# Attention rows: the output product in a score bank behind the turning, the keys copied by VectorE

## The reference

```python
x = _layernorm(pair_rep, gamma, beta)
q = x @ Wq * C ** (-0.5)
k = (x @ Wk).reshape(n, s, s, H, C)
v = (x @ Wv).reshape(n, s, s, H, C)
dpa = jnp.einsum('nsqhc,nsvhc->nsqvh', k, q)
pair_bias = x @ Wb
dpa = dpa + bias[:, None, :, :, None]
attention = jax.nn.softmax(dpa + pair_bias[:, None], axis=3)
out = jnp.einsum('nsqvh,nsvhc->nsqhc', attention, v)
fu = jax.nn.sigmoid(x @ Wu + bu)
out = out * fu
out = out.reshape(n, s, s, H * C) @ Wo + bo
out = out * mask[..., None]
```

## Time and profile before

| | us |
|---|---|
| median of 3 runs | 2528.18 (2527.36 to 2529.87) |
| profiled execution, its own time | 2533.66 |
| its span in the trace | 2531.9 |
| attention rows (76 to 428 us of the span) | 352 |
| PE busy, whole span | 2199.2 |
| DVE busy, whole span | 2185.8 |
| ACT busy, whole span | 1763.2 |
| POOL busy, whole span | 2075.4 |

### The profile page before, as it was taken

One profiled execution on the slowest core, in us unless ns is written; L12 is line 12 of the kernel. 1 busy time (PEld: TensorE's weight loads), 2 busy tenths in 40 slices (PEclk: granted clock), 3 DMA queues, 4 the chain that ended last, 5 costly groups with the idle time before them and its releaser, 6 DMA issues. The chain is left out here.

```text
span 2531.9 us, 36914 instructions
## 1 busy us (share of the span) xinstructions
PE 2199.2 (87%) x9081; PEld 1134.5 (45%) x9158; DVE 2185.8 (86%) x2247; ACT 1763.2 (70%) x3999; POOL 2075.4 (82%) x1330
## 2 busy tenths in 40 slices
PE   6899997776898889988999889999899999988798
PEld 6566664463444444444444333333344333333543
DVE  5677777535999999999999999999999999998796
ACT  4799997566878778787788755656555656553487
POOL 4455555204999999999999999999999999999489
PEclk9999998786999999999999999999989999989899
DMA  4000000005677766776676777777777767765022
GB/s 71 14 12 12 12 12 8 1 1 139 214 232 227 225 232 223 236 226 224 228 228 234 234 241 247 239 231 241 237 230 246 241 231 243 237 224 183 13 60 63
DMA packets 192552, 421.07 MB, mean 166 GB/s; under 512 B 66548, under 2 KB 95705, under 8 KB 192474
## 3 DMA queue, kind: packets, MB, share of 16 engines
q1 hardware_dynamic: 190938, 416.01, 52.1%
q10 hardware_dynamic: 1536, 4.20, 0.5%
HBM read 387.63 MB, written 24.12 MB: 163 GB/s over the span
## 5 line engine op out<-in xcount | busy, mean ns | idle before, releaser
L1589 POOL TENSOR_TENSOR s_hc<-s_h,s_cc 128x1024 f32<-128x1024 f32 x512 | 1200.8, 2363 | 61.2 <-PE s_py L1342 45.4
L1342 PE MATMUL s_py<-s_hc,ident 128*128 128x512 f32 x2048 | 991.6, 609 | 14.9 <-DVE s_yo L1635 14.5
L1672 DVE TENSOR_TENSOR_SCAN s_h<-s_dA,s_state,s_pu 128x1024 f32<-128x1024 f32 x330 | 770.3, 2342 | 27.7 <-PE s_pu L1320 4.7
L1342 PEld LDWEIGHTS s_py<-s_hc,ident 128*128 128x128 f32 x2048 | 389.9, 195 | 386.5 <-issue 314.6
L1503 ACT ACTIVATE s_dA<-s_dt,ss_A 128x1024 f32<-128x1024 f32 x352 | 401.6, 1142 | 9.2 <-ACT s_brow L1459 7.8
L1508 ACT ACTIVATE s_pu<-s_dt,ss_A 128x1024 f32<-128x1024 f32 x160 | 178.4, 1115 | 322.5 <-DVE s_h L1672 317.0
L1582 POOL TENSOR_TENSOR s_dbx<-s_dtx,s_bb 128x1024 f32<-128x1024 f32 x160 | 377.8, 2362 | 2.5 <-DVE s_dtx L1627 2.5
L1672 DVE TENSOR_TENSOR_SCAN s_h<-s_pu,s_state,s_dbx 128x1024 f32<-128x1024 f32 x150 | 350.2, 2335 | 21.2 <-ACT s_pu L1508 19.8
L1648 DVE TENSOR_TENSOR s_pu<-s_pu,s_dtx 128x1024 f32<-128x1024 f32 x288 | 349.1, 1212 | 15.8 <-PE s_pu L1329 13.5
L1329 PE MATMUL s_pu<-s_bcs,ss_sel 128*128 128x512 bf16 x499 | 163.5, 398 | 121.4 <-DVE s_h L1672 117.2
L588 POOL TENSOR_TENSOR ar_ex<-ar_ex,ar_rs 128x512 f32<-128x512 f32 x128 | 133.0, 1039 | 158.3 <-DVE ar_rs L537 158.2
(11 more groups left out here) (289 smaller groups left out, 3587.0 us busy)
## 6 DMA issues: line engine op xcount, KB each, us to landing
s_cc<-rows_scratch SPq DMA_DIRECT2D x512, 512.0 KB, 4.6
s_bb<-rows_scratch SPq DMA_DIRECT2D x160, 512.0 KB, 4.9
s_n<-n_scratch SPq DMA_DIRECT2D x64, 258.0 KB, 5.6
y_scratch<-s_yo SPq DMA_DIRECT2D x16, 512.0 KB, 5.4
s_yf<-y_scratch SPq DMA_DIRECT2D x16, 512.0 KB, 5.8
x_tok<-in_x_dram SPq DMA_DIRECT2D x16, 256.0 KB, 4.5
at_xg<-at_xT SPq DMA_DIRECT2D x64, 64.0 KB, 2.1
n_scratch<-ss_turned SPq DMA_DIRECT2D x32, 128.0 KB, 4.2
```

The source lines that it names most:

```text
L1342: ins = nc.tensor.matmul(p_y[:, hf], lhsT=c.ident[:, :], rhs=hc[:, s % RING, hf], start=(s == 0), stop=(s == U - 1))
L1589: nc.gpsimd.tensor_tensor(hc[:, s % RING, :], h[:, s % RING, :], cc[:, s % C_RING, :], ALU.mult).then_inc(read, 1)
L1672: nc.vector.tensor_tensor_scan(out=flow(h[:, s % RING, :]), data0=flow(decays), data1=flow(inputs), initial=begun, op0=ALU.mult, op1=ALU.a ...
```

## The change

y moves from `ps_o` to the first score bank: `ps_s[:, 0, 128:192]`. With that `attend` no longer waits for `x_done`, `score` waits for the `x_done` of row r-6, since it writes into y's bank, and `project_output` waits for `added` of its own step, since DVE's addition of the bias reads that bank. `project_output` stands right behind `turn`, ahead of `values` and of the projection. On DVE, `add_to_x` works on row r-5 in place of r-6 and stands behind `apply_gate`, ahead of the reciprocal. `take_k` moves from ACT, position 3, to DVE, position 2, behind `take_values`.

```diff
--- before.py
+++ after.py
@@ -417,7 +417,7 @@
         ps_t = ctx.enter_context(nc.psum_tensor("ar_pst", [128, 512], F32))
         ps_o = ctx.enter_context(nc.psum_tensor("ar_pso", [128, 512], F32))
         p_s = ps_s[:, :, 0:128]
-        o_T, p_y = ps_o[:, 0:128], ps_o[:, 128:128 + D]
+        o_T, p_y = ps_o[:, 0:128], ps_s[:, 0, 128:128 + D]
         sem = lambda n: c.sem("ar_" + n)
 
         (q_made, k_made, u_made, q_taken, k_taken, u_taken) = (
@@ -461,8 +461,10 @@
                 nc.tensor.matmul(ps_p[:, :], lhsT=wvu[:, 128:256], rhs=xg[:, k, :], start=True,
                                  stop=True).then_inc(u_made, 1)
 
-            def project_output(r, j, next_attended):
-                pe.wait_ge(gated, r + 2 if next_attended else r + 1)
+            def project_output(r, j, scores_read):
+                pe.wait_ge(gated, r + 1)
+                if scores_read is not None:
+                    pe.wait_ge(added, scores_read + 1)
                 need(pe, x_done, r)
                 nc.tensor.matmul(p_y, lhsT=og[:, j % 2, :], rhs=wo[:, :], start=True, stop=True).then_inc(y_made, 1)
 
@@ -489,7 +491,6 @@
                 pe.wait_ge(e_taken, r + 1)
                 pe.wait_ge(v_taken, r + 1)
                 need(pe, gated, r)
-                need(pe, x_done, r - 1)
                 for h in range(HEADS):
                     ins = nc.tensor.matmul(ps_o[band[h], 0:128], lhsT=va[:, k, j, band[h]], rhs=exT[:, j % 2, tile(h)],
                                            start=True, stop=True)
@@ -499,11 +500,14 @@
 
                 if has(0):
                     need(pe, added, r)
+                    need(pe, x_done, r - 5)
                     score(r, j, g, k)
                 if has(4):
                     attend(r - 4, j, 1 - k)
                 if has(3):
                     turn(r - 3, (j - 3) % GR)
+                if has(5):
+                    project_output(r - 5, (j - 5) % GR, r if has(0) else None)
                 if has(0):
                     values(r, j, k)
                 if pair is not None:
@@ -513,8 +517,6 @@
                         project_k(g + 1, 1 - k)
                     if j == 3:
                         project_u(g + 1, 1 - k)
-                if has(5):
-                    project_output(r - 5, (j - 5) % GR, has(4))
             project_q(0, 0, 0)
             project_k(0, 0)
             project_u(0, 0)
@@ -550,23 +552,31 @@
                 nc.vector.scalar_tensor_tensor(out=xr, in0=p_y, scalar=maskT[:, bass.ds(r, 1)], in1=xr,
                                                op0=ALU.mult, op1=ALU.add).then_inc(x_done, 1)
 
+            def take_k(g, k):
+                dve.wait_ge(k_made, g + 1)
+                need(dve, scored, GR * (g - 1))
+                nc.vector.tensor_copy(kT[:, k, :], ps_p[:, :]).then_inc(k_taken, 1)
+
             def take_values(r, j, k):
                 dve.wait_ge(v_made, r + 1)
                 need(dve, o_made, r - 2 * GR + 1)
                 nc.vector.tensor_copy(va[:, k, j, :], ps_v[:, 0:128]).then_inc(v_taken, 1)
 
             def step(r, j, g, k, has, pair):
-                if has(6):
-                    add_to_x(r - 6)
                 if has(0):
                     add_bias(r, j)
                 if has(4):
                     apply_gate(r - 4, j, g - 1, 1 - k)
+                if has(5):
+                    add_to_x(r - 5)
                 if has(2):
                     invert_sums(r - 2, (j - 2) % GR)
                 if has(0):
                     minimum(r, j)
                     take_values(r, j, k)
+                if pair is not None and j == 2:
+                    take_k(g + 1, 1 - k)
+            take_k(0, 0)
             row_steps(dve, step)
             dve.wait_ge(x_done, S)
 
@@ -603,11 +613,6 @@
                 need(act, scored, GR * (g - 1))
                 nc.scalar.activation(qT[:, k, :], ps_p[:, :], ACT.Copy, scale=-SCALE).then_inc(q_taken, 1)
 
-            def take_k(g, k):
-                act.wait_ge(k_made, g + 1)
-                need(act, scored, GR * (g - 1))
-                nc.scalar.copy(kT[:, k, :], ps_p[:, :]).then_inc(k_taken, 1)
-
             def take_u(g, k):
                 act.wait_ge(u_made, g + 1)
                 need(act, gated, GR * (g - 1))
@@ -634,12 +639,9 @@
                     take_u(g, k)
                 if pair is not None and j == 2:
                     take_q(g + 1, 1 - k)
-                if pair is not None and j == 3:
-                    take_k(g + 1, 1 - k)
                 if has(3):
                     take_turned(r - 3, (j - 3) % GR)
             take_q(0, 0)
-            take_k(0, 0)
             take_u(0, 0)
             row_steps(act, step)
```

## The result

| | before | after |
|---|---|---|
| median, us (4 runs each) | 2529.02 | 2564.02 |
| range of the runs, us | 2527.36 to 2532.20 | 2562.90 to 2566.23 |
| ratio, 95% interval | | 1.0138 (1.0120 to 1.0155) |
| span of the profiled execution, us | 2531.9 | 2561.3 |
| last addition to x of the attention rows ends, us | 427.4 | 459.7 |

The attention rows end 32.3 us later. Of that, 30 groups at 1.01 us are 30 us. The drain, from the start of the last scores to the start of the last addition to x, takes 13.6 us instead of 11.2. The remainder of the program, from that start on, has the same instructions and took 2104.8 us in the profiled execution of before and 2101.9 in that of after, so the two spans differ by 29.4 us. In the twelve other profiled executions of this study that remainder lies between 2095.7 and 2107.1 us, 11 us apart.

What follows compares the result with a forecast made beforehand. In the attention row loop neither PE nor ACT alone was taken as the bound; a ring of waits would lengthen 30 groups from 10.86 to 11.79 us, 28 us, less 1: +27 on 2528.18 gives 2555 us, range 2537 to 2565.

Steps and rivals of the forecast that it cites:

- the ring: Attention row loop: closed chain of waits over four rows through PE, DVE, POOL and ACT, 11.79 us against 10.86.
- (a): DVE to PE: from the start of the bias addition (L528) to the output product that waits for it, 0.81 us.
- (b): On PE: from the output product through values and projection to the next scores, 1.34 us.
- (c): PE and DVE: from scores through the bias addition (L528) to output, 1.38 us at position 2 or 1.47 at 0.
- (d): From output through DVE's addition to x and reciprocal, POOL's scaling and PE's turn to the next output, 2.64 us.
- (e): From output through DVE's addition to x and minimum, ACT's exponentials and q copy to PE's k projection, 3.84 us.
- (f): From PE's k projection through DVE's keys copy to the next bias addition (L528), 1.69 us.
- POOL's ring: Row loop: the output-to-output path through POOL's scaling repeated at all four positions, 4 x 2.64 = 10.56 us a group.
- Rival B: Row loop: q is taken in time, so DVE's own way decides; group 11.27 us, +12 us, 2540; chance 0.14.
- the ceiling: Attend's wait for the addition to x: removing 0.24 us for each of 128 rows gains at most about 30 us.
- Rival C: Row loop: the removed wait wins, k and q copies never late; group 10.56 us, -9 us, 2519; chance 0.08.
- Rival E (the clock): Attention stage: more PE idle time lowers the granted clock, adding 24 us or more, 2580; chance 0.06.

Runs made afterwards that it cites:

- e3: The changed kernel with DVE's addition to x moved behind the reciprocal, still ahead of the minimum: 2554.80 us, 1.0103 of the kernel before.
- e5: The changed kernel with ACT's q copy moved ahead of the exponentials at position 2: 2550.36 us, 1.0069 of the kernel before.
- e4: The changed kernel with DVE's addition to x moved behind reciprocal and minimum, ahead of the values copy: 2538.55 us, 1.0036 of the kernel before.
- e2: The changed kernel with the keys copy put back on ACT at position 3: 2560.01 us, 1.0119 of the kernel before.
- e12: The changed kernel with the addition to x behind the minimum and the keys copy back on ACT: 2533.04 us, 1.0017 of the kernel before.
- e6: The changed kernel with y back in its old bank, the new orders kept: 2579.37 us, 1.0187 of the kernel before.
- e9: The kernel before with turn ahead of attend, DVE's reciprocal ahead of the bias addition, and ACT's four copies ahead of the exponentials: 2529.50 us, ratio 0.9991.
- e10: The kernel before with only the output product moved ahead of the projection, behind values: 2519.79 us, ratio 0.9960.
- e7: The kernel before with only the values product moved ahead of attend and turn on PE: 2529.88 us, ratio 0.9997.

## Why the prediction was right, and where it was off

**The sign, the ring and its members held.** 2555 was forecast with 2537 to 2565; 2564 was measured. The size is less good than that sounds: 2564 is 1 us inside the range and 1 us above the band that I gave to my own case (2545 to 2563), and 35 us were measured where 27 were forecast. All of the waits that I named are there, that of the k projection with 0.5 us in 30 cases where I had 0.6 in 31. One sign of being wrong showed by its letter: the minimum starts 0.29 us behind the addition to x (206.24 to 206.53) and I had written 0.3. The legs had 0.31 there, so the bound was drawn too tight; the waits behind it are as forecast. The ring's sum was 11.79 us a group and the trace has 11.87. Leg by leg, from the rows of after:

| leg | forecast | measured |
|---|---|---|
| (a) L528 to output, position 3 | 0.81 | 0.73 (211.17 to 211.90) |
| (b) output to the scores of position 0 | 1.34 | 1.51 (211.90 to 213.41) |
| (c) scores to output, position 0 | 1.47 | 1.40 (213.41 to 214.81) |
| (d) through POOL to output, position 1 | 2.64 | 2.72 (214.81 to 217.53) |
| (e) through ACT to the k projection | 3.84 | 3.74 (205.66 to 209.40) |
| (f) through the keys copy to L528 | 1.69 | 1.77 (209.40 to 211.17) |
| sum | 11.79 | 11.87 |

That the sum is within 0.08 us is in part luck, since errors of both signs, up to 0.17 us in a leg, cancel. In (a) the wake-up is 0.05 and not 0.12: the weight load itself waits. In (b) output to values is 0.28, values to projection 0.27 and projection to scores 0.96, where the earlier trace rows gave 0.26, 0.22 and 0.86 for other neighbours. In (d) output to the addition to x is 0.68 at a step where output had waited, 0.58 otherwise. The unknown price, the keys copy on DVE, was estimated at 0.68 and is 0.69; the next instruction follows after 0.61, not 0.60.

**The groups and the drain.** 30 groups were right; at 1.01 us they give 30 us. The last step of the sum failed: I took 1 us off for the start and the drain, and the drain is 2.4 us longer. Each drained row of after passes through POOL's ring too: its turns start 2.48, 2.49 and 3.09 us apart (446.97, 449.45, 451.94 and 455.03, each held by POOL), where those of before start 2.03, 1.87 and 1.86 apart (416.96 to 422.72). Of these 2.3 us the ring has 1.7. The other 0.6 is the clock: the last of the three steps runs at the lower level and takes 3.09 instead of 2.49, all of it in PE's own work (the turn shows as 1.11 us instead of 0.65). In before the clock kept its higher level through those steps and fell only behind them, at about 425 us (stretch, busy us, clock, DMA; before, then after):

```profile
410.00:422.00 12.00, 9.97 (x124) 7.36 (x124) 9.31 (x31) 10.52 (x45) 8.64 (x18) 1.00 0.01 2
422.00:428.00 6.00, 3.10 (x26) 2.09 (x26) 1.65 (x6) 0.72 (x2) 0.81 (x2) 0.75 0.01 3
```

```profile
440.00:451.00 11.00, 7.82 (x92) 5.50 (x90) 7.62 (x26) 9.89 (x42) 6.43 (x13) 1.00 0.00 0
451.00:460.00 9.00, 5.88 (x40) 4.06 (x40) 2.08 (x8) 1.17 (x3) 2.73 (x5) 0.52 0.01 2
```

With the group and the drain as measured the prediction would have been 2561 (2528.2 and 30.3 and 2.4). The last 3 us to the median are within what the rest of the program moves from one execution to the next, and I don't explain them.

**The legs were tested one by one.** e3 took POOL's leg, e5 ACT's, e4 both, e2 and e12 the keys copy, and every group came out within some 0.1 us of what was expected from its legs once the change had been measured. Rival B (11.27) is e5 at 11.41.

**The rule on banks.** The Trainium skill, PSUM — Partial Sum Buffer, section PSUM bank collisions raise a hardware error, has engines kept apart by bank and not by address, and by it the wait in (a) is unavoidable. No run here leaves the wait out, so none shows a collision. The price of the wait in the trace is 12.3 us of idle in 56 cases before output's weight load, and in e6 the other bank's wait, for the gate, is the dearer one (28.6 us in 76 cases, from 90 to 400 us).

**What failed beside the sum: the ceiling.** "The most to be had is about 30 us" and PE's 9.90 us a group (2.69 and 1.83 a step) counted idle time as if the work on both sides kept its price in any order. e9 to e12 show steps without idle of 2.79 to 2.82 us. Scores to attend, which I had at 0.50 without the idle, is 0.43 in e10 and e12; the rest of their step is dearer. And the 10.2 us of the weight loads that I added to the 26.2 of the products in the earlier trace rows are the same wait seen twice, though the 30 us did not use them. Rival C (2519) rested on this floor and on POOL's ring of 10.56; e12, the kernel closest to its premise, has 11.04, and there the scores of position 1, behind the step without a projection, wait for the addition to x. The same 0.35 us stand before the scores of position 1 in the rows of after (204.01 and 215.88). I had given that new wait of the scores no term at all. It did not matter for the forecast because POOL's ring was longer there. In e12 it is 0.38 of 11.04 us, more than the 0.18 by which that group is longer than before; no kernel without it was run.

**Rival E (the clock)** fell for the loop: the granted clock was 1.00 up to 451 us with the added idle times. In the drain it came true on a small scale, with the 0.6 us above. I had read the clock of the drain from 424 to 430 us; the steps ahead of 424 us, which are most of it, had the higher level.

## What to carry to other kernels

When an instruction that waits for a late result is moved up in an in-order queue, price what now stands behind it, not the instruction: here an addition of 0.28 us, which waits 0.5 to 0.7 us for y, ahead of a reciprocal and a minimum cost 25 us, since POOL, ACT and in the end PE itself hung on these two. Follow such a chain until it closes; a ring's length, summed from the distances between starts, gave the new period within 1%. And an idle time on a busy TensorE can be worth less than it shows, and a TensorE that shows no idle time can still be waiting (e7): try the smallest reorder (here one call moved up by one place) before banks and engines are changed.

## What the runs showed of the hardware

The price of a product on PE depends on what stands before and behind it. The values product (128 x 128 float32, two passes) took 0.22 us to the next instruction behind transposes, 0.27 to 0.28 behind the output product, and 0.42 behind scores; the output product 0.17 to 0.37; a projection 0.86 us before output (0.96 in e7, where it had waited) and 0.96 to 1.01 before scores. The price goes with how far the product's first weight load begins ahead of it: for values 0.11 us ahead in before (0.22 us), 0.06 in after (0.27) and not at all in e7 (0.42). Four orders of the same products, none with an idle time, ended at 2.79, 2.82, 2.82 and 2.82 us a step. The Trainium skill, TensorE: Matmul & The Clock Gate, section Back-to-back issue gap, says that the spacing of a stream is set by weight loads and products together; the trace agrees: a weight load shows as 0.19 us where the two passes of the values product take 0.22 to the next instruction at best, and the same product is dearer where its load is not ahead.

DVE copies 512 float32 columns out of PSUM in 0.69 us, as long as an addition of two operands takes, and ACT in 0.56 to 0.59.
